# The first mixture's router stage in another order: expert loads and first splits earlier, token halves made there, slot weights summed between the gather's matmuls

## The chip, the cores and the metric

One core of a Trainium2 chip runs the whole program. The metric is the device time of one execution in microseconds (us). TensorE (PE) does matrix products, VectorE (DVE), ScalarE (ACT) and GpSimd (POOL) elementwise work, and SyncE (SP) issues the transfers.

## The reference

Two layers on 1024 tokens of 256 channels. The part around the change is the start of layer 0, cut here to what matters:

```
xn = layernorm(x)
s  = attention(xn, wq, wk, wv, wo)          # 16 heads of 128
# mixture of 32 experts, 4 per token, capacity C = 40 slots each
scores = sigmoid(xn @ router_w.T)
groups = top 3 of 8 groups by (scores + bias); idx = top 4 experts in them
w      = 2.5 * scores[idx] / sum(scores[idx])
Xp     = xn[slots_token]                    # (32 experts, 40 slots, 256)
Y      = (silu(Xp @ W_gate) * (Xp @ W_up)) @ W_down
out    = scatter_add(Y * slots_w) + (silu(xn @ shared_gate.T) * (xn @ shared_up.T)) @ shared_down.T
x      = x + s * silu(out)
```

## The kernel before

All operands stay in SBUF. Tokens lie on 128 partitions in 8 tiles (NT = 8). Products that need more than half precision are made of float16 halves: a value is split into a high half (a cast) and a low half (value minus high), and three products are summed.

The program is a row of blocks. In a block each engine has its own instruction stream, ordered by semaphores alone; at a block's end all five engines, SP too, meet at a barrier. Four blocks matter:

- **The first norm** (`layer_norm`, called from `route0` at L252): DVE normalizes, PE transposes `xn`, ACT copies the transposes to `xnT`. SP meanwhile issues five transfers (`load_first`, L247 to L251).
- **The router block** (L254 to L431). PE: `router_w` is turned, the logits follow (L273), the three shared weights are turned (L281), and four steps of the shared expert's gate and up products run (`shared_gate_up`, L292; a step is four float32 products, and the trace has two records for each). Two steps stand before the wait for `sel_ready`, then the counting products `pos` (L302, L303), then the other two steps. The gather (L316, L318) multiplies `xn` halves by the 0/1 matrix `member`, 12 products per token tile. The sums of slot weights `ws` (L325, L326, 160 small products) come last. DVE: one chain (`Chain`: each operation waits for the one before) computes the selection from `prob` (L389) to `sel16` (L407), then weights and places (L408 to L419), then the 8 tiles of `member` (L421), the low halves `xg_l` of the gathered tokens (L427) and the slot weights (L429, L431). ACT: sigmoid, copies of the turned weights, per shared step a Silu and a copy, and per expert of the first eight a high half and a scaled copy (`weights_high`, L343, L345). POOL: the halves of `xn` (L371, L373), per shared step a product `shared_hT` (L378), and per expert a low half (`weights_low`, L367). SP: 24 loads for experts 0 to 7 at the block's start, three for each of experts 8 to 15 once the buffer is free.
- **The expert block** (`experts0`): 32 experts; PE's products, ACT's `e_sg`, `e_hh`, and DVE's `e_hf`, `e_hl` follow each other per expert. POOL makes the halves of `xnT` for the attention that comes later (L559, L561); that is all it does there.
- **The combination** (`combine0`), and then the attention.

The order of work on each engine is written out by hand; nothing schedules it.

Of the kernel before, what the change touches and what calls it, by code (L numbers as in the profile page):

```python
# [7 lines left out]
ALU = mybir.AluOpType  # L8
ACT = mybir.ActivationFunctionType
# [4 lines left out]
NT = T // P  # L14
D = 256
DC = D // P
HALF = 512
# [12 lines left out]
ST = SLOTS // P  # L30
# [176 lines left out]
def route0(nc, env, router_w, e_bias):  # L207
# [6 lines left out]
    with ExitStack() as local:  # L214
# [20 lines left out]
        member_ready, gathered, xg_done, ws_ready, wm_done = (sem("r0_" + s) for s in ("me", "ga", "xg", "ws", "wm"))  # L235
        high_done, xn_split = (sem("r0_" + s) for s in ("hi", "xn"))
        wf, w_h, w_l, w_high, w_ready = (env[k] for k in ("wf", "w_h", "w_l", "w_high", "w_ready"))
# [9 lines left out]
        def load_first(sp):  # L247
            sp.dma_start(rw[:, :], router_w).then_inc(loaded[0], 16)
            sp.dma_start(bias[:, :], e_bias.partition_broadcast(P)).then_inc(loaded[1], 16)
            for i, src in enumerate(env["shared_weights"]):  # L250
                sp.dma_start(w3[i][:, :, :], src.rearrange("(a p) d -> p a d", p=P)).then_inc(w3_loaded[i], 16)  # L251
        layer_norm(nc, env, "ln0", env["x"], env["xn"], xnT, loads=load_first, side=env["fill_masks"])  # L252

        with nc.Block() as block:  # L254
            @block.sync
            def _(sp):

                for e in range(EB):
                    load_expert(sp, env, e, e)
                for b in range(EB):  # L260
                    sp.wait_ge(w_ready, b + 1)
                    load_expert(sp, env, EB + b, b)

            @block.tensor
            def _(pe):
# [29 lines left out]

                for step in range(2 * IC - 2):
                    shared_gate_up(step)
# [6 lines left out]
                last.then_inc(pos_ready, 1)  # L304
                for step in range(2 * IC - 2, 2 * IC):
                    shared_gate_up(step)

                pe.wait_ge(up_done, 2 * IC)
                pe.wait_ge(xn_split, 1)
                for n in range(NT):  # L310
                    pe.wait_ge(member_ready, n + 1)
                    for c in range(DC):
                        for k, (at, size) in enumerate(cuts):
# [6 lines left out]
                            if n == NT - 1:  # L320
                                last.then_inc(gathered, 1)
                for s in range(ST):
                    for n in range(NT):
                        slots = member[:, n, :, :].rearrange("p e c -> p (e c)")[:, s * P:(s + 1) * P]
                        pe.matmul(ws[:, s, :], slots, wk_h[:, n, :], start=(n == 0), stop=False)  # L325
                        last = pe.matmul(ws[:, s, :], slots, wk_l[:, n, :], start=False, stop=(n == NT - 1))  # L326
                last.then_inc(ws_ready, 1)

            @block.scalar
            def _(act):  # L330
                act.wait_ge(rwT_ready, 1)
                act.activation(rwT[:, :, :], turned, ACT.Copy).then_inc(rwT_done, 1)
                act.wait_ge(logits_ready, 1)
# [6 lines left out]
                def weights_high(e):  # L340

                    act.wait_ge(env["expert_loaded"][e], 48)
                    act.activation(w_h[e][:, :, :], wf[e][:, :, :], ACT.Copy, scale=WSCALE).then_inc(w_high, 1)  # L343
                    act.wait_ge(w_high, 2 * e + 1)
                    act.activation(wf[e][:, :, :], wf[e][:, :, :], ACT.Copy, scale=WSCALE).then_inc(w_high, 1)  # L345

                for step in range(2 * IC):
                    act.wait_ge(gu_ready, step + 1)
                    if step >= 2:
                        act.wait_ge(h_ready, step - 1)  # L350
                    bank = 2 * (step % 2)
                    act.activation(sg[:, step % 2, :], psum[:, bank, :], ACT.Silu).then_inc(silu_done, 1)
                    act.activation(up[:, step % 2, :], psum[:, bank + 1, :], ACT.Copy).then_inc(up_done, 1)
                    weights_high(step)
                for e in range(2 * IC, EB):
                    weights_high(e)
                for c in range(DC):
                    for k, (at, size) in enumerate(cuts):
                        bank = c * len(cuts) + k
                        act.wait_ge(gathered, bank + 1)  # L360
                        act.activation(xg_h[:, c, at:at + size], psum[:, bank, 0:size], ACT.Copy).then_inc(xg_done, 1)

            @block.gpsimd
            def _(pool):
                def weights_low(e):
                    pool.wait_ge(w_high, 2 * e + 2)
                    pool.tensor_tensor(w_l[e][:, :, :], wf[e][:, :, :], w_h[e][:, :, :], ALU.subtract).then_inc(w_ready, 1)  # L367
# [4 lines left out]
                pool.wait_ge(high_done, 1)  # L372
                pool.tensor_tensor(xn_l[:, :, :], xn[:, :, :], xn_h[:, :, :], ALU.subtract).then_inc(xn_split, 1)  # L373
                for step in range(2 * IC):
                    t, ic = step // IC, step % IC
                    pool.wait_ge(silu_done, step + 1)
                    pool.wait_ge(up_done, step + 1)
                    pool.tensor_tensor(hT[:, ic, t * HALF:(t + 1) * HALF], up[:, step % 2, :], sg[:, step % 2, :],  # L378
                                       ALU.mult).then_inc(h_ready, 1)
                    weights_low(step)  # L380
                for e in range(2 * IC, EB):
                    weights_low(e)

# [50 lines left out]
EB = 8  # L434
# [13 lines left out]
def experts0(nc, env):  # L448

    sem, psum, xg_h, xg_l, yT, wf, loaded = (env[k] for k in ("sem", "psum", "xg_h", "xg_l", "yT", "wf", "expert_loaded"))  # L450
    w_h, w_l, w_ready, xnT = (env[k] for k in ("w_h", "w_l", "w_ready", "xnT"))
    with ExitStack() as local:
        def tmp(name, shape, dt=F32):
# [3 lines left out]
        h_h, h_l = ([tmp(f"{n}{b}", [P, CAP], F16) for b in range(BANKS)] for n in ("hh", "hl"))  # L457
        wh_ready, gu_ready, silu_done, h_ready, hh_ready, hl_ready, y_ready, y_done, x_high = (
            sem("e0_" + s) for s in ("nwh", "gu", "si", "h", "hh", "hl", "y", "yd", "xh"))

# [13 lines left out]
        with nc.Block() as block:  # L474
# [57 lines left out]
            def _(dve):  # L532
# [20 lines left out]
                rounds(dve, (0, hidden, False), (3, next_low, True), (0, hidden_low, False), (3, outputs, False))  # L553

            @block.gpsimd
            def _(pool):

                high, low = env["xT_h"], env["xT_l"]
# [1654 lines left out]
```

## Time and profile before

| | |
|---|---|
| time, median of 3 runs | 1448.96 us (1448.11 to 1452.94) |
| span of the profiled execution, first to last instruction | 1450.3 us |
| router block, in that execution | about 15.1 to 73.2 us |
| expert block | from 73.5 us on |
| busy over the whole span | PE 87%, DVE 71%, ACT 50%, POOL 37% |

The profiled execution's own time is not listed apart from its span, which lies inside the range of the three runs and 1.3 us above their median. Times in the rows below count from the span's start.

### The profile page before, as it was taken

Reading aid. Unit: us, or ns where it says so; the run is one execution under the profiler, and the core shown is the slowest. Engines: PE = TensorE matmul, PEld = TensorE weight load, DVE = VectorE, ACT = ScalarE, POOL = GpSimd, SP = SyncE. Lnnn points to the kernel's source line nnn. Section 1 sums busy time; section 2 is a strip of 40 time slices with the busy share of each in tenths; the row PEclk is TensorE's granted clock in tenths of the full one; section 3 lists DMA queues with packets and bytes.
Section 4 is the critical chain, followed back from the end, with each engine's and each line's share of the span. In section 5 each row is a group of like instructions: output and inputs, shape, how many; then the busy total and the mean of one; then the engine's idle time right before and its main releaser. Section 6 shows DMA issues by size and latency. Waiting matters only on the chain. (4 is left out here: it accounts for less than half of the span.)

```text
span 1450.3 us, 25230 instructions
## 1 busy us (share of the span) xinstructions
PE 1258.0 (87%) x8970; PEld 764.3 (53%) x8970; DVE 1029.5 (71%) x1516; ACT 731.9 (50%) x1313; POOL 539.8 (37%) x333
## 2 busy tenths in 40 slices
PE   6857689988889988888998888796676999999997
PEld 4556556665665666565666547552233454444443
DVE  4785178998989998989998871459964425555554
ACT  3462376776676676676576641343035413434443
POOL 3612244546544545544454400034434003333332
PEclk9956899999999999999999999788888999999999
DMA  4351000000000000000000100103000024434441
GB/s 139 88 168 30 22 1 12 12 12 11 0 11 11 11 11 11 0 11 11 11 0 0 58 0 2 37 0 111 0 0 1 0 70 124 119 113 127 116 112 61
DMA packets 66543, 59.21 MB, mean 41 GB/s; under 512 B 7057, under 2 KB 61825, under 8 KB 66497
## 3 DMA queue, kind: packets, MB, share of 16 engines
q1 hardware_dynamic: 66496, 58.59, 14.1%
q8 instruction: 29, 0.48, 0.1%
q14 instruction: 18, 0.14, 0.0%
HBM read 57.26 MB, written 1.31 MB: 40 GB/s over the span
## 5 line engine op out<-in xcount | busy, mean ns | idle before, releaser
L1094 DVE SCALAR_TENSOR_TENSOR a_pr<-a_ex,a_rtot,a_pr 128x1024 f16<-128x1024 f32 x128 | 214.7, 1677 | 4.5
L1023 ACT COPY a_pT<-psum 128x1024 f32<-128x1024 f32 x128 | 130.6, 1020 | 93.6 <-PE psum L920 93.6
L1013 ACT ACTIVATE a_ex<-psum,a_nmax 128x1024 f32<-128x1024 f32 x128 | 144.9, 1132 | 65.2 <-DVE a_nmax L1079 65.2
L2074 POOL TENSOR_TENSOR e_sg<-e_sg,e_cb 128x512 f32<-128x512 f32 x64 | 82.0, 1282 | 242.2 <-ACT e_sg L2022 242.2
L1079 DVE TENSOR_REDUCE a_nmax<-psum 128x1 f32<-128x1024 f32 x128 | 155.4, 1214 | 19.6 <-PE psum L910 19.5
L1092 DVE TENSOR_SCALAR a_pr<-a_ex,a_rtot 128x1024 f16<-128x1024 f32 x128 | 161.8, 1264 | 5.1
L920 PE MATMUL psum<-ident,a_pr 128*128 128x128 f16 x2048 | 144.0, 227 | 24.2 <-DVE a_pr L1094 23.4
L920 PEld LDWEIGHTS psum<-ident,a_pr 128*128 128x128 f16 x2048 | 129.5, 102 | 42.0 <-DVE a_pr L1094 35.7
L851 POOL TENSOR_TENSOR a_qkTl<-a_qkTf,a_qkTh 128x512 f16<-128x512 f32 x64 | 93.1, 1473 | 100.6 <-ACT a_qkTf L997 100.6
L892 PE MATMUL psum<-a_wh,xT_h 128*128 128x128 f16 (+1 forms) x512 | 114.6, 247 | 3.0 <-PEq L578 1.2
L831 POOL TENSOR_TENSOR a_rnorm<-a_ss,a_power 128x16 f32<-128x16 f32 x16 | 46.4, 2903 | 188.8 <-DVE a_ss L1071 188.8
L893 PE MATMUL psum<-a_wl,xT_h 128*128 128x128 f16 (+1 forms) x512 | 114.5, 247 | 0.0
L894 PE MATMUL psum<-a_wh,xT_l 128*128 128x128 f16 (+1 forms) x512 | 114.5, 247 | 0.0
L2030 ACT ACTIVATE e_hh<-e_hf 128x512 f16<-128x512 f32 x64 | 40.3, 630 | 143.4 <-DVE e_hf L2099 143.4
L935 PE MATMUL psum<-a_pT,a_vh 128*128 128x512 f16 x256 | 97.0, 379 | 1.1 <-ACT a_pT L1023 1.1
L1945 PE MATMUL psum<-xT_h,e_guh 128*128 128x512 f16 x256 | 97.0, 379 | 0.4 <-DVE e_hf L2099 0.4
L936 PE MATMUL psum<-a_pT,a_vh 128*128 128x512 f16 x256 | 97.0, 379 | 0.0
L937 PE MATMUL psum<-a_pT,a_vl 128*128 128x512 f16 x256 | 97.0, 379 | 0.0
L1947 PE MATMUL psum<-xT_h,e_gul 128*128 128x512 f16 x256 | 97.0, 379 | 0.0
L1946 PE MATMUL psum<-xT_l,e_guh 128*128 128x512 f16 x256 | 97.0, 379 | 0.0
L880 PE MATMUL psum<-ident,qk 128*128 128x128 f32 x256 | 42.0, 302 | 50.0 <-ACT a_qkTf L997 19.4
L906 PE MATMUL psum<-a_qkTh 128*128 128x512 f16 x256 | 80.3, 397 | 0.0
(355 smaller groups left out, 2991.4 us busy)
## 6 DMA issues: line engine op xcount, KB each, us to landing
e_cb<-comb_by_expert SPq DMA_DIRECT2D x64, 256.0 KB, 3.7
wf<-in_L_ffn_W_gate SPq DMA_DIRECT2D x32, 128.0 KB, 2.3
wf<-in_L_ffn_W_up SPq DMA_DIRECT2D x32, 128.0 KB, 2.4
wf<-in_L_ffn_W_down SPq DMA_DIRECT2D x32, 128.0 KB, 2.9
e_guf<-in_L_ffn_wg SPq DMA_DIRECT2D x32, 128.0 KB, 2.2
e_guf<-in_L_ffn_wu SPq DMA_DIRECT2D x32, 128.0 KB, 2.2
e_dnf<-in_L_ffn_wd SPq DMA_DIRECT2D x32, 128.0 KB, 2.1
a_wf<-in_L_attn_wq SPq DMA_DIRECT2D x16, 128.0 KB, 2.2
```

Source lines behind the costliest of these rows:

```text
L892: pe.matmul(dst, xh, wh, start=(c == 0), stop=False)
L893: pe.matmul(dst, xh, wl, start=False, stop=False)
L894: last = pe.matmul(dst, xl, wh, start=False, stop=(c == DC - 1))
L920: last = pe.transpose(out, pr[m % 2][:, part, k * P:(k + 1) * P], ident16[:, :])
L935: pe.matmul(out, v_h[b][:, k, :], ph, start=(k == 0), stop=False)
L936: pe.matmul(out, v_h[b][:, k, :], pl, start=False, stop=False)
L937: last = pe.matmul(out, v_l[b][:, k, :], ph, start=False, stop=(k == KT - 1))
L1013: act.activation(ex[m % 2][:, :], psum[:, bank:bank + 2, :].rearrange("p a b -> p (a b)"), ACT.Exp, bias=nmax[:, m % 2:m % 2 + 1], accum_o ...
L1023: act.copy(dst, src).then_inc(pT_ready, 1)
L1079: dve.tensor_reduce(nmax[:, m % 2:m % 2 + 1], psum[:, bank:bank + 2, :].rearrange("p a b -> p (a b)"), AX.X, ALU.max, negate=True).then_in ...
L1092: dve.tensor_scalar(pr[k][:, 0, :], ex[k][:, :], rtot[:, k:k + 1], None, ALU.mult).then_inc(ph_ready, 1)
L1094: dve.scalar_tensor_tensor(pr[k][:, 1, :], ex[k][:, :], rtot[:, k:k + 1], pr[k][:, 0, :], ALU.mult, ALU.subtract).then_inc(p_ready, 1)
```

## The change

- The 24 loads of experts 0 to 7 are issued in the first norm's block, behind its five transfers.
- In the router block ACT splits expert 0 (high half) and makes `xT_h` before the sigmoid, and splits experts 1 and 2 before the first shared step; the other splits move up by three experts.
- POOL makes the low half of expert 0, then `xT_l` in four pieces of 512, then the low halves of experts 1 and 2, before the first shared product. The expert block loses both POOL operations.
- PE runs three shared steps before the counting products, and one after.
- The slot weight sums are made per token tile behind that tile's gather products.

```diff
 # route0, load_first (in the first norm's block)
                 sp.dma_start(w3[i][:, :, :], src.rearrange("(a p) d -> p a d", p=P)).then_inc(w3_loaded[i], 16)
+            for e in range(EB):
+                load_expert(sp, env, e, e)
 # router block, SP
-                for e in range(EB):
-                    load_expert(sp, env, e, e)
 # PE
-                for step in range(2 * IC - 2):
+                for step in range(2 * IC - 1):
                     shared_gate_up(step)
                 pe.wait_ge(sel_ready, 1)
...
-                for step in range(2 * IC - 2, 2 * IC):
-                    shared_gate_up(step)
+                shared_gate_up(2 * IC - 1)
...
-                for s in range(ST):
-                    for n in range(NT):
+                    for s in range(ST):
-                        pe.matmul(ws[:, s, :], slots, wk_h[:, n, :], start=(n == 0), stop=False)
+                        pe.matmul(ws[:, s, :], slots, wk_h[:, n, :], start=(n == 0 and s == 0), stop=False)
 # ACT
+                weights_high(0)
+                act.activation(env["xT_h"][:, :, :], xnT[:, :, :], ACT.Copy).then_inc(xT_high, 1)
                 act.wait_ge(logits_ready, 1)
...
+                weights_high(1)
+                weights_high(2)
                 for step in range(2 * IC):
...
-                    weights_high(step)
-                for e in range(2 * IC, EB):
-                    weights_high(e)
+                    weights_high(3 + step)
+                weights_high(EB - 1)
 # POOL
+                weights_low(0)
+                pool.wait_ge(xT_high, 1)
+                for c in range(DC):
+                    for half in range(2):
+                        at = (slice(None), c, slice(half * HALF, (half + 1) * HALF))
+                        pool.tensor_tensor(env["xT_l"][at], xnT[at], env["xT_h"][at], ALU.subtract)
+                weights_low(1)
+                weights_low(2)
                 for step in range(2 * IC):
...
-                    weights_low(step)
-                for e in range(2 * IC, EB):
-                    weights_low(e)
+                    weights_low(3 + step)
+                weights_low(EB - 1)
 # experts0, POOL
-                pool.tensor_copy(high[:, :, :], xnT[:, :, :]).then_inc(x_high, 1)
-                pool.wait_ge(x_high, 1)
-                pool.tensor_tensor(low[:, :, :], xnT[:, :, :], high[:, :, :], ALU.subtract)
```

SP's queue around the barrier between the norm's block and the router block, before (the branch that waits for the barrier opens the router block; `wf` are the experts' weights):

```order
L251 DMA r_w<-in_L_ffn_shared_down 128x2x256
L144 UNCONDITIONAL_BRANCH
L255 UNCONDITIONAL_BRANCH [waits barrier_Pool_Activation_PE_DVE_SP_release]
L442 DMA wf<-in_L_ffn_W_gate 128x256
L442 DMA wf<-in_L_ffn_W_up 128x256
```

The same place now, with the last six of the 24 expert loads ahead of the barrier:

```order
L449 DMA wf<-in_L_ffn_W_gate 128x256
L449 DMA wf<-in_L_ffn_W_up 128x256
L451 DMA wf<-in_L_ffn_W_down 128x256
L449 DMA wf<-in_L_ffn_W_gate 128x256
L449 DMA wf<-in_L_ffn_W_up 128x256
L451 DMA wf<-in_L_ffn_W_down 128x256
L144 UNCONDITIONAL_BRANCH
L257 UNCONDITIONAL_BRANCH [waits barrier_Pool_Activation_PE_DVE_SP_release]
```

So 24 transfers that were issued behind the barrier are issued ahead of it.

POOL's queue from the router block's start, before (`wl` are the experts' low halves; the expert block begins at L555):

```order
L371 CAST xn_h<-xn 128x2048
L373 TENSOR_TENSOR xn_l<-xn,xn_h 128x2048
L378 TENSOR_TENSOR shared_hT<-r_up,r_sg 128x512
L367 TENSOR_TENSOR wl<-wf,wh 128x768
L378 TENSOR_TENSOR shared_hT<-r_up,r_sg 128x512
L367 TENSOR_TENSOR wl<-wf,wh 128x768
L378 TENSOR_TENSOR shared_hT<-r_up,r_sg 128x512
L367 TENSOR_TENSOR wl<-wf,wh 128x768
L378 TENSOR_TENSOR shared_hT<-r_up,r_sg 128x512
L367 TENSOR_TENSOR wl<-wf,wh 128x768 x5
```

And now:

```order
L371 CAST xn_h<-xn 128x2048
L373 TENSOR_TENSOR xn_l<-xn,xn_h 128x2048
L367 TENSOR_TENSOR wl<-wf,wh 128x768
L379 TENSOR_TENSOR xT_l<-xnT,xT_h 128x512 x4
L367 TENSOR_TENSOR wl<-wf,wh 128x768 x2
L386 TENSOR_TENSOR shared_hT<-r_up,r_sg 128x512
L367 TENSOR_TENSOR wl<-wf,wh 128x768
L386 TENSOR_TENSOR shared_hT<-r_up,r_sg 128x512
L367 TENSOR_TENSOR wl<-wf,wh 128x768
```

Seven operations (three `wl`, four pieces of `xT_l`) now stand between `xn_l` and the first `shared_hT`, where nothing stood.

PE's queue around the counting products, as a difference:

```order
 L273 MATMUL psum<-r_rwT,xnT 128x32 x16
 L281 MATMUL psum<-ident,r_w 128x128 x12
-L292 MATMUL psum<-xnT,shared_wT 128x512 x8
+L292 MATMUL psum<-xnT,shared_wT 128x512 x12
 L303 MATMUL psum<-r_sel,upper 128x32
 L302 MATMUL psum<-r_sel,ones 128x32
```

Four products, one shared step, moved ahead of the counting products.

## Rows read from the trace of the kernel before

**Rows 1.** Busy time by stage: us, engine busy (instructions), granted clock, DMA share, GB/s.

```profile
50.60:68.00 17.40, 17.36 (x98) 9.46 (x99) 12.29 (x7) 9.44 (x14) 16.04 (x7) 1.00 0.39 115
...
80.00:120.00 40.00, 24.88 (x516) 21.65 (x514) 33.86 (x115) 27.12 (x82) 0.00 (x0) 0.50 0.53 159
```

**Rows 2.** Timeline, start of the router block: start, duration, engine, operation [idle before].

```profile
6.94 0.47 SPq L251 DMA_DIRECT2D r_w<-in_L_ffn_shared_down  x1
...
13.98 0.81 ACT L175 ACTIVATE xnT<-psum 128x256 f32<-128x256 f32 x2 [0.41 <-PE psum L190]
15.06 0.34 SPq L442 DMA_DIRECT2D wf<-in_L_ffn_W_gate  x1
...
17.05 4.06 POOL L373 TENSOR_TENSOR xn_l<-xn,xn_h 128x2048 f16<-128x2048 f32 x1
...
25.88 0.43 SPq L444 DMA_DIRECT2D wf<-in_L_ffn_W_down  x1
```

**Rows 3.** Timeline, ACT before the sigmoid.

```profile
22.88 0.39 ACT L334 ACTIVATE r_prob<-psum 128x256 f32<-128x256 f32 x1 [5.83 <-PE psum L273]
```

**Rows 4.** Timeline, DVE and POOL while the selection is computed.

```profile
33.63 1.27 POOL L378 TENSOR_TENSOR shared_hT<-r_up,r_sg 128x512 f32<-128x512 f32 x1 [12.52 <-ACT r_up L353]
...
34.25 0.69 DVE L201 COPY r_named<-r_best 128x32 f32<-128x32 f32 x1
...
37.34 1.13 DVE L204 TENSOR_SCALAR r_sel<-r_er 128x256 f32<-128x256 f32 x1
...
38.60 1.70 POOL L367 TENSOR_TENSOR wl<-wf,wh 128x768 f16<-128x768 f32 x1 [0.28 <-ACT wf L345]
38.72 1.87 DVE L408 TENSOR_TENSOR r_w<-r_prob,r_sel 128x256 f32<-128x256 f32 x1
```

**Rows 5.** One line's instructions, `member` and `wl`: shortest, median and longest in ns.

```profile
L421 DVE TENSOR_TENSOR member<-r_place,steps x8: 1481/2554/2932, 44.1 to 59.0; 128x1280 f16<-128x1280 f32 x8
...
L367 POOL TENSOR_TENSOR wl<-wf,wh x8: 1632/2296/2894, 35.2 to 65.0; 128x768 f16<-128x768 f32 x8
```

**Rows 6.** Timeline, three places of DVE's chain.

```profile
23.30 0.43 DVE L389 TENSOR_TENSOR r_sc<-r_prob,r_bias 128x256 f32<-128x256 f32 x1 [11.51 <-ACT r_prob L334]
...
24.99 0.23 DVE L396 TENSOR_TENSOR r_lo<-r_sums 128x64 f32<-128x64 f32 x1
...
44.14 17.80 DVE L421 TENSOR_TENSOR member<-r_place,steps 128x1280 f16<-128x1280 f32 x8
```

**Rows 7.** Timeline, PE: shared steps, counting products, gather and slot weight sums.

```profile
26.14 9.65 PE L292 MATMUL psum<-xnT,shared_wT 128*128 128x512 f32 x16 [0.69 <-ACT shared_wT L337]
...
38.86 0.21 PE L303 MATMUL psum<-r_sel,upper 128*128 128x32 f16 x1 [3.06 <-DVE r_sel L407]
...
39.84 9.62 PE L292 MATMUL psum<-xnT,shared_wT 128*128 128x512 f32 x16
...
50.64 0.39 PE L316 MATMUL psum<-member,xn_h 128*128 128x512 f16 x1 [1.18 <-ACT r_up L353]
...
67.96 0.18 PE L325 MATMUL psum<-wk_h,member 128*128 128x32 f16 x1
...
71.93 0.18 PE L326 MATMUL psum<-wk_l,member 128*128 128x32 f16 x1
```

**Rows 8.** Stretches around the counting products; columns as in group 1.

```profile
40.00:42.00 2.00, 2.00 (x4) 0.97 (x4) 1.83 (x6) 0.00 (x0) 0.30 (x1) 0.50 0.21 65
...
44.00:46.00 2.00, 2.00 (x5) 0.85 (x4) 1.97 (x3) 0.00 (x0) 0.00 (x0) 0.78 0.00 0
```

**Rows 9.** Timeline, DVE at the router block's end.

```profile
67.05 3.14 DVE L427 TENSOR_TENSOR xg_l<-psum,xg_h 128x512 f16<-128x512 f32 x6 [5.11 <-ACT xg_h L361]
...
72.67 0.49 DVE L431 TENSOR_REDUCE w_slot<-r_wmask 128x10 f32<-128x320 f32 x1
```

**Rows 10.** Timeline, POOL and DVE in the expert block.

```profile
75.43 4.06 POOL L561 TENSOR_TENSOR xT_l<-xnT,xT_h 128x2048 f16<-128x2048 f32 x1
...
75.94 3.60 DVE L540 TENSOR_TENSOR e_hl<-e_hf,e_hh 128x40 f16<-128x40 f32 x1 [0.30 <-ACT e_hh L522]
```

More of the change, by code:

```diff
@@ L235, in route0 @@
         member_ready, gathered, xg_done, ws_ready, wm_done = (sem("r0_" + s) for s in ("me", "ga", "xg", "ws", "wm"))
-        high_done, xn_split = (sem("r0_" + s) for s in ("hi", "xn"))
+        high_done, xn_split, xT_high = (sem("r0_" + s) for s in ("hi", "xn", "xh"))
         wf, w_h, w_l, w_high, w_ready = (env[k] for k in ("wf", "w_h", "w_l", "w_high", "w_ready"))
@@ L321, in _ @@
                                 last.then_inc(gathered, 1)
-                for s in range(ST):
-                    for n in range(NT):
+                    for s in range(ST):
                         slots = member[:, n, :, :].rearrange("p e c -> p (e c)")[:, s * P:(s + 1) * P]
-                        pe.matmul(ws[:, s, :], slots, wk_h[:, n, :], start=(n == 0), stop=False)
-                        last = pe.matmul(ws[:, s, :], slots, wk_l[:, n, :], start=False, stop=(n == NT - 1))
+                        pe.matmul(ws[:, s, :], slots, wk_h[:, n, :], start=(n == 0 and s == 0), stop=False)
+                        last = pe.matmul(ws[:, s, :], slots, wk_l[:, n, :], start=False, stop=(n == NT - 1 and s == ST - 1))
                 last.then_inc(ws_ready, 1)
@@ L332, in _, with weights_high @@
                 act.activation(rwT[:, :, :], turned, ACT.Copy).then_inc(rwT_done, 1)
+                def weights_high(e):
+                    act.wait_ge(env["expert_loaded"][e], 48)
+                    act.activation(w_h[e][:, :, :], wf[e][:, :, :], ACT.Copy, scale=WSCALE).then_inc(w_high, 1)
+                    act.wait_ge(w_high, 2 * e + 1)
+                    act.activation(wf[e][:, :, :], wf[e][:, :, :], ACT.Copy, scale=WSCALE).then_inc(w_high, 1)
+                weights_high(0)
+                act.activation(env["xT_h"][:, :, :], xnT[:, :, :], ACT.Copy).then_inc(xT_high, 1)
                 act.wait_ge(logits_ready, 1)
@@ L338, in _ @@
                                    ACT.Copy).then_inc(wT_done, 1)
[L340 to L345, printed above, removed]
+                weights_high(1)
+                weights_high(2)
                 for step in range(2 * IC):
@@ L450, in experts0 @@
     sem, psum, xg_h, xg_l, yT, wf, loaded = (env[k] for k in ("sem", "psum", "xg_h", "xg_l", "yT", "wf", "expert_loaded"))
-    w_h, w_l, w_ready, xnT = (env[k] for k in ("w_h", "w_l", "w_ready", "xnT"))
+    w_h, w_l, w_ready = (env[k] for k in ("w_h", "w_l", "w_ready"))
     with ExitStack() as local:
@@ L457, in experts0 @@
         h_h, h_l = ([tmp(f"{n}{b}", [P, CAP], F16) for b in range(BANKS)] for n in ("hh", "hl"))
-        wh_ready, gu_ready, silu_done, h_ready, hh_ready, hl_ready, y_ready, y_done, x_high = (
-            sem("e0_" + s) for s in ("nwh", "gu", "si", "h", "hh", "hl", "y", "yd", "xh"))
+        wh_ready, gu_ready, silu_done, h_ready, hh_ready, hl_ready, y_ready, y_done = (
+            sem("e0_" + s) for s in ("nwh", "gu", "si", "h", "hh", "hl", "y", "yd"))
         def rounds(engine, *jobs):
@@ L553, in _ @@
                 rounds(dve, (0, hidden, False), (3, next_low, True), (0, hidden_low, False), (3, outputs, False))
-            @block.gpsimd
-            def _(pool):
-                high, low = env["xT_h"], env["xT_l"]
-                pool.tensor_copy(high[:, :, :], xnT[:, :, :]).then_inc(x_high, 1)
-                pool.wait_ge(x_high, 1)
-                pool.tensor_tensor(low[:, :, :], xnT[:, :, :], high[:, :, :], ALU.subtract)
 def combine0(nc, env):
```

## The prediction, made before the changed kernel ran

> **What bounds the kernel now.** I read the busy time by stage first, then the timeline of each engine through the router block. The whole program is serial by blocks, so a microsecond in the router block or in the expert block is one of the total. In the router block the bound changes hands. First PE: from the barrier to the sigmoid's inputs, for which ACT sat idle 5.83 us [rows 3]. Then DVE's selection chain, from 23.3 to 38.8 [rows 4, 6]: PE stood idle 3.06 us before the counting products because `sel16` wasn't there [rows 7]. Then PE again: two shared steps of 9.62 us in all, at first at the lower clock, a wait of 1.18 us for ACT, then the gather from 50.64 to 67.96 and the slot weights to 71.96 [rows 7]; the stage row shows PE busy 17.36 of 17.40 us and DVE with room [rows 1]. A short DVE tail ends the block at 73.16 [rows 9]. In the expert block one DVE operation of 40 columns took 3.60 us [rows 10].
>
> **Term 1, the barrier: +3.9.** SP meets the barrier too. Its last transfer of the norm's block was issued by 7.41, and the barrier fell when ACT was through at 14.79; the next block began at 15.06, 0.27 later [rows 2]. The 24 loads took from 15.06 to 26.31, 0.469 us each [rows 2]. Behind 7.41 they end at 7.41 + 24 x 0.469 = 18.7, so the router block begins at about 19.0 and not at 15.06: +3.9 us. Nothing of it comes back by itself: no engine in the router block waited for an expert load before (the waits there are for PE and for DVE [rows 3, 7]). If SP issued faster ahead of a barrier, the least is 0; the most is the row's value.
>
> **Term 2, work put ahead of the sigmoid on ACT: 0.** The split of expert 0 and `xT_h` lie in ACT's idle 5.83 us before the sigmoid [rows 3], with the table load: I estimate some 1.7 + 2.0 us. Experts 1 and 2 are split while PE does shared step 0. Without that cover the first would cost 3.7 us.
>
> **Term 3, POOL against DVE: +10.5.** This is the large one. The timeline of both engines [rows 4] shows that certain DVE operations do not run beside a POOL operation: the copy of 32 columns begun at 34.25 took 0.69 us and ended with POOL's product (34.90); `r_sel` took 1.13 us; the product begun at 38.72 took 1.87 us and ended just after POOL's `wl` (40.30). The subtraction of 40 columns in the expert block lasted until POOL's 4.06 us operation was over [rows 10]. When both queues are full they take turns: the longest `member` is 2.93 against 1.48 us for the shortest, so one `wl` of 1.63 us costs DVE 1.45 [rows 5], 0.89 of its length.
>
> Now POOL had nothing between 21.11 and 33.63 [rows 2, 4], just where DVE's chain begins. After the change, with everything 3.9 later, `xn_l` ends at 25.0, `wl` of expert 0 at 26.7, and then four pieces of `xT_l` follow (about 1.15 us each, between a quarter of the 4.06 and the 1.27 of another operation on 512 columns [rows 10, 4]), then two `wl`. DVE's chain begins at 27.2, and its first six operations, 23.30 to 25.22 before [rows 6], each have two inputs in SBUF. Each waits for one POOL operation and lets the next one in when it ends: 0.6 us of the first piece, 3 x 1.0 for the others, 2 x 1.45 for the `wl` of experts 1 and 2 (ready at about 31.7 and 33.4, POOL comes to them at 32.0 and 33.7): 6.5 us.
>
> The rest of the chain is now later against the shared steps. PE's steps 0, 1 and 2 end at 36.2, 39.7 and 43.1 ([rows 7], 3.9 later, the third step at the faster half's pace of about 3.4 us), so POOL has `shared_hT` and `wl` three times between 37.6 and 47.6. DVE's maxima and match operations run through; stepping through the others I find five waits: 1.0, 1.05, 1.2, 0.9 and 1.3 us, together 5.4. All six POOL operations by 0.89 of their lengths would be 7.7, none 0. Taken away are the old waits of this kind before `sel16`: 0.5 and 0.85 us [rows 4]. So `sel16` is ready at 38.8 + 3.9 + 6.5 + 5.4 - 1.35 = 53.2. The bounds of this term: -1.35, if nothing contends any more, and +12.9.
>
> The Trainium skill bears on this, in "SBUF — State Buffer", section "Who interferes with whom": a VectorE instruction with two SBUF inputs and a GpSimd instruction that reads SBUF exclude each other for the whole instruction. The rows agree that they exclude each other; with the whole length in place of 0.89 of it, the sum would be 1.3 us higher.
>
> **Term 4, the shared step moved: -3.4.** Step 2 fills PE until 43.1, then PE is idle ten microseconds. The counting products take 1.0 us as before (38.86 to 39.84 [rows 7]), to 54.2. Before, after 3.06 us of idling, the granted clock was 0.50, 1.2 GHz, and 0.78 as a mean at 44 to 46 [rows 8], and two steps took 9.62 us, where at 2.4 GHz they would be twice 3.4. After a longer idle time I expect the same start: one step of 6.2 us, 3.4 less than the two (about 6.4 of its 8 records at the slow pace of 0.86 us). It ends at 60.4. The wait for ACT stays 1.2: the gather begins at 61.6 instead of 50.64. `member` doesn't hold it: the chain from 38.72 to 44.14 [rows 4, 6] is 1.45 us shorter without the old wait, so the tiles start at 57.2 and the third is ready by 61.5.
>
> **Term 5, slot weights beside the gather: +1.5.** PE had to do 17.3 us of gather and 4.0 of slot weights [rows 7]; interleaved it does the same 21.3, since `member`'s tiles come faster than the 2.66 us it then needs for one. Gather and sums end at 82.9. What changes is the tail. Before, DVE's `xg_l`, 3.14 us long and ended at 70.19, lay beside the slot weight sums, which ended at 71.96, and the block ended 1.2 later at 73.16 [rows 7, 9]. `xg_l` ended 4.4 us after the last tile's gather began (a tile is 17.3 / 8 = 2.17 us, so that was at 65.8). Now that tile begins 2.67 before PE's end, so `xg_l` ends 1.7 after it, and the two slot weight operations of 0.49 us each follow: 2.75. The block ends at 85.7 against 73.16: +12.5. Were PE waiting for `member`, the sums would be free and this term would be a gain of up to 2.5.
>
> **Term 6, the expert block: -3.4.** Without POOL's subtraction the 3.60 us operation takes 0.2, as its like do [rows 10]. DVE is the busiest engine there, 33.86 of 40 us [rows 1], and the whole pipeline starts by that much earlier. Least 0, most 4.1.
>
> **Sum.** 3.9 + (6.5 + 5.4 - 1.35) gives `sel16` 14.4 later; PE gets back 3.4 (one step less behind it), gathers 11.0 later, ends 1.5 later in the tail (12.5), and gains 3.4: +9.1 us. The span of the profiled execution, 1450.3, would be 1459.4; the three runs have a median 1.3 lower, so I predict 1449.0 + 9.1 = 1458.1, and 0.6% slower.
>
> **Rivals.**
> *The contention is small (chance 0.13; on the other side).* If DVE's short operations pass between POOL's, `sel16` comes at 38.8 + 3.9 - 1.35 = 41.4, before PE is through with step 2 at 43.1. Then PE never idles: counting to 43.8, step 3 to 47.2, gather from 48.4 to 69.7, end at 72.4. With the expert block that is -0.8 - 3.4 = -4.2: 1444.8. For it: the maxima and match operations don't wait. Against it: every overlap of the two engines that I looked at [rows 4, 5, 10]. It decides from the point where all waits together stay under about 2 us: `sel16` by 43.4 gives a gather at 51.8 even with a slow step 3, and at most no loss.
> *Half of it (0.16).* POOL's operations fall beside maxima and match operations more than I stepped: waits of 6 us. `sel16` at 47.3, PE cold, gather from 55.7, the end at 79.8: +6.6 - 3.4 = +3.2: 1452.2, with a spread of 1450.5 to 1455.
> *The clock in the expert block (0.06).* It is 0.50 from 80 to 120 [rows 1] and fell beside the stall that goes. Should it stay at 2.4 GHz, the block can shrink until DVE is full, by at most 40.0 - 33.9 = 6.1: 1452.0. Against it: PE is not the bound there, and its idle time before that block grows from 1.9 to over 3 us. With little contention as well it would be 1439; I count half of the 0.06 for each.
>
> **How the numbers follow.** The main case has 0.65 and its own range is 1455 to 1462 (terms 3 and 4 each off by 2 to 3). From 1450 to 1462 I take in the half case and most of the clock case, and leave out the rival on the other side: 0.8 in all. What a measurement can tell from no change is about 0.3%, 4.3 us, so from 1444.6 to 1453.3. Slower: the main case and half of the half case, 0.65 + 0.08 = 0.73. Faster: 0.08 of the small contention, which lies at the very bound, and 0.03 of the clock case, 0.11. Within: the rest, 0.16.
>
> **What would show it.** The router block's first operation at 19.0 and not 15.1. `r_sc`, `r_hi`, `r_lo` and their kind each at 1.0 to 1.8 us instead of 0.3, with POOL's `xT_l` ending where they end. The counting products near 54, after a PE idle time of some ten microseconds, and slow records in step 3. The gather from about 61.6 and 21.3 us long, `xg_l` behind PE's end. The `e_hl` group without its 3.60. The prediction is wrong if DVE's first six operations keep their 0.3 us, if SP's issues are not waited for, or if PE waits for `member` tile by tile.

## The result, and the profile after

| | before | changed |
|---|---|---|
| median (range) of 15 runs each | 1448.56 us (1445.40 to 1453.73) | 1455.13 us (1453.35 to 1456.37) |
| span of the profiled execution | 1450.3 | 1452.6 |

The ratio is 1.0037, 95% interval 1.0026 to 1.0047: the changed kernel is slower by 5.4 us (3.8 to 6.8). The medians lie 6.6 us apart; the means of the same runs, 1449.49 and 1454.93 us, 5.4. Predicted were 9.1 us and a time of 1458.1, with a range of 1450 to 1462.

The two spans differ by 2.3 us only. One line's instructions in the attention show where the two executions part. These are ACT's copies `sq`, in the kernel before:

```profile
L985 ACT ACTIVATE sq<-psum x64: 597/597/605, 164.3 to 798.7; 128x512 f32<-128x512 f32 x64
```

and in the changed one:

```profile
L984 ACT ACTIVATE sq<-psum x64: 597/597/604, 170.0 to 801.9; 128x512 f32<-128x512 f32 x64
```

The attention starts 5.7 us later and ends 3.2 later, with the same code. Over all thirteen traces of this study the same distance runs from 631.9 us (the changed kernel has this) to 634.8; before has 634.4. So an execution can lose or gain up to 2.9 us there for no cause in the kernel. I compare the stages ahead of the attention in the traces, and the totals by the ratio.

Start of the router block after the change, timeline of SP, POOL and ACT:

```profile
18.41 0.43 SPq L451 DMA_DIRECT2D wf<-in_L_ffn_W_down  x1
19.25 1.89 POOL L371 CAST xn_h<-xn 128x2048 f16<-128x2048 f32 x1 [11.74 <-POOLq L144]
21.23 4.07 POOL L373 TENSOR_TENSOR xn_l<-xn,xn_h 128x2048 f16<-128x2048 f32 x1
25.25 1.64 POOL L367 TENSOR_TENSOR wl<-wf,wh 128x768 f16<-128x768 f32 x1
...
26.85 4.78 POOL L379 TENSOR_TENSOR xT_l<-xnT,xT_h 128x512 f16<-128x512 f32 x4
...
27.06 0.39 ACT L341 ACTIVATE r_prob<-psum 128x256 f32<-128x256 f32 x1 [2.42 <-PE psum L273]
...
31.96 3.25 POOL L367 TENSOR_TENSOR wl<-wf,wh 128x768 f16<-128x768 f32 x2 [0.33 <-ACT wf L336]
```

Against [rows 2] the barrier falls 4.2 us later, behind SP's last issue; POOL's 7.55 us of idle time in the norm's block became 11.74. ACT still idles 2.42 us for PE before the sigmoid [rows 3]: what was put there is hidden.

DVE's chain in the same timeline:

```profile
27.48 0.81 DVE L396 TENSOR_TENSOR r_sc<-r_prob,r_bias 128x256 f32<-128x256 f32 x1 [15.70 <-ACT r_prob L341]
28.32 1.13 DVE L399 TENSOR_TENSOR r_hi<-r_sc 128x128 f32<-128x128 f32 x1
29.49 1.12 DVE L400 TENSOR_TENSOR r_lo<-r_sc 128x128 f32<-128x128 f32 x1
30.65 1.13 DVE L401 TENSOR_TENSOR r_sums<-r_hi,r_lo 128x128 f32<-128x128 f32 x1
31.81 0.23 DVE L402 TENSOR_TENSOR r_lo<-r_hi 128x64 f32<-128x64 f32 x1
32.07 1.61 DVE L403 TENSOR_TENSOR r_lo<-r_sums 128x64 f32<-128x64 f32 x1
...
33.98 1.30 DVE L405 TENSOR_TENSOR r_gs<-r_lo 128x64 f32<-128x64 f32 x1
...
40.99 4.47 DVE L411 TENSOR_TENSOR r_es<-r_sc,r_gm 128x64 f32<-128x64 f32 x4
...
50.76 0.29 DVE L414 CAST r_sel<-r_sel 128x256 f16<-128x256 f32 x1
...
54.94 15.29 DVE L428 TENSOR_TENSOR member<-r_place,steps 128x1280 f16<-128x1280 f32 x8
```

`r_hi`, `r_lo` and `r_sums` took 0.29 us each before and take 1.13 now, nearly as long as one piece of `xT_l` (4.78 us for four). The one operation of the six that kept its 0.23 is the one that came while POOL idled 0.33 us for ACT. `sel16` is ready at 51.05, 12.25 us later than before [rows 4].

PE's timeline, against [rows 7]:

```profile
30.32 10.57 PE L292 MATMUL psum<-xnT,shared_wT 128*128 128x512 f32 x24 [0.69 <-ACT shared_wT L344]
51.11 0.21 PE L303 MATMUL psum<-r_sel,upper 128*128 128x32 f16 x1 [10.22 <-DVE r_sel L414]
...
52.10 4.59 PE L292 MATMUL psum<-xnT,shared_wT 128*128 128x512 f32 x8
...
57.87 0.39 PE L315 MATMUL psum<-member,xn_h 128*128 128x512 f16 x1 [1.18 <-DVE member L428]
...
79.17 0.18 PE L324 MATMUL psum<-wk_l,member 128*128 128x32 f16 x1
```

PE idles 10.22 us for `sel16` and gathers 7.2 us later than before. Gather and sums take 21.5 us together, as before. Busy time and granted clock of the changed kernel in three stretches around the last step, and at the end one in the expert block (columns as in [rows 1]; the clock column, the third from the end, is 0.50 at 1.2 GHz and 1.00 at 2.4 GHz):

```profile
50.00:52.00 2.00, 0.89 (x33) 0.89 (x34) 1.83 (x8) 0.00 (x0) 0.00 (x0) 0.50 0.00 0
52.00:54.00 2.00, 2.00 (x13) 0.97 (x10) 1.83 (x6) 0.00 (x0) 0.00 (x0) 0.51 0.00 0
54.00:56.00 2.00, 2.00 (x6) 0.91 (x5) 1.90 (x4) 0.00 (x0) 0.00 (x0) 1.00 0.00 0
...
88.00:128.00 40.00, 25.20 (x493) 21.79 (x491) 32.45 (x110) 25.91 (x78) 0.13 (x2) 0.50 0.55 165
```

DVE's tail and the expert block, against [rows 9, 10]:

```profile
77.79 3.15 DVE L434 TENSOR_TENSOR xg_l<-psum,xg_h 128x512 f16<-128x512 f32 x6 [7.55 <-ACT xg_h L361]
...
81.36 0.49 DVE L438 TENSOR_REDUCE w_slot<-r_wmask 128x10 f32<-128x320 f32 x1
...
84.73 0.20 DVE L547 TENSOR_TENSOR e_hl<-e_hf,e_hh 128x40 f16<-128x40 f32 x1 [0.30 <-ACT e_hh L529]
...
127.54 0.48 DVE L635 TENSOR_SCALAR c_yw_h<-psum,w_slot 128x256 f16<-128x256 f32 x1 [2.01 <-PE psum L599]
```

The block ends at 81.85 instead of 73.16; the 3.60 us operation is 0.20. The last row is the combination's first DVE operation. It began at 121.94 before. So up to there the change costs 5.6 us in these two executions, which is the size of the measured difference.

### The profile page after: what moved, and what is told of

Its sections match the earlier page's. It is cut to its first block and busy times, and to the rows that moved or that the text cites. A ratio compares the mean times of both kernels' runs of the same rounds, so it can differ in the third digit from the quotient of the medians.

```text
span 1452.6 us, 25233 instructions
## 1 busy us (share of the span) xinstructions
PE 1249.9 (86%) x8970; PEld 761.9 (52%) x8970; DVE 1034.3 (71%) x1516; ACT 733.8 (51%) x1314; POOL 531.8 (37%) x335
## 5 line engine op out<-in xcount | busy, mean ns | idle before, releaser
L1091 DVE TENSOR_SCALAR a_pr<-a_ex,a_rtot 128x1024 f16<-128x1024 f32 x128 | 165.9, 1296 | 5.1
L919 PE MATMUL psum<-ident,a_pr 128*128 128x128 f16 x2048 | 143.2, 226 | 24.1 <-DVE a_pr L1093 23.4
L830 POOL TENSOR_TENSOR a_rnorm<-a_ss,a_power 128x16 f32<-128x16 f32 x16 | 46.4, 2902 | 190.4 <-DVE a_ss L1070 190.4
L879 PE MATMUL psum<-ident,qk 128*128 128x128 f32 x256 | 42.4, 304 | 49.9 <-ACT a_qkTf L996 19.4
L2098 DVE SCALAR_TENSOR_TENSOR e_hf<-psum,e_sg 128x512 f32<-128x512 f32 x64 | 43.8, 684 | 50.3 <-POOL e_sg L2073 50.3
```

The source lines that it names most:

```text
L919: last = pe.transpose(out, pr[m % 2][:, part, k * P:(k + 1) * P], ident16[:, :])
L1091: dve.tensor_scalar(pr[k][:, 0, :], ex[k][:, :], rtot[:, k:k + 1], None, ALU.mult).then_inc(ph_ready, 1)
```

## The experiments

The places that tell the runs apart, in us from each span's start. "Combination" is the first `c_yw_h`; the ratio is to runs of the kernel before on the same chip, with its 95% interval. Ten or more runs stand behind each ratio, but only five behind the last one. The places are of one execution each.

| kernel | chain starts | sel16 | member starts | block ends | combination | ratio |
|---|---|---|---|---|---|---|
| before | 23.3 | 38.8 | 44.1 | 73.2 | 121.9 | 1 |
| changed | 27.5 | 51.05 | 54.9 | 81.9 | 127.5 | 1.0037 (1.0026, 1.0047) |
| before + loads early | 27.5 | 42.8 | 48.1 | 77.1 | 125.8 | 1.0027 (1.0010, 1.0043) |
| changed, loads back | 23.4 | 47.3 | 51.2 | 79.0 | 124.05 | 1.0007 (0.9996, 1.0019) |
| changed, xT_l out | 27.5 | 46.4 | 50.3 | 77.5 | 123.2 | 1.0002 (0.9987, 1.0017) |
| changed, splits back | 27.5 | 46.0 | 51.3 | 77.6 | 123.2 | 1.0003 (0.9990, 1.0016) |
| changed, loads back, xT_l out | 23.7 | 44.2 | 48.1 | 76.2 | 121.1 | 0.9984 (0.9975, 0.9993) |
| before + sums beside | 23.3 | 38.1 | 43.4 | 73.0 | 121.8 | 0.9998 (0.9985, 1.0011) |
| before + step moved | 23.3 | 38.7 | 48.3 | 75.8 | 124.6 | 0.9992 (0.9979, 1.0005) |
| before + xT out | 23.3 | 39.05 | 44.4 | 71.8 | 116.75 | 0.9971 (0.9952, 0.9991) |
| the same, again | 23.3 | 40.7 | 44.6 | 74.5 | 120.2 | 0.9984 (0.9972, 0.9996) |
| mix | 23.3 | 41.6 | 45.5 | 73.1 | 118.2 | 0.9980 (0.9965, 0.9995) |
| mix, low halves late | 23.3 | 39.7 | 43.6 | 70.5 | 116.2 | 0.9955 (0.9942, 0.9969) |

The theory after the result: the barrier costs 4.2 us, POOL's operations ahead of and among DVE's chain cost more than that, and a gain in PE's steps and in the expert block gives a part back. The rival: the loads or the clock made the chain or PE late, and POOL is a bystander.

**The loads alone (kernel before).**

```diff
 # load_first
                 sp.dma_start(w3[i][:, :, :], src.rearrange("(a p) d -> p a d", p=P)).then_inc(w3_loaded[i], 16)
+            for e in range(EB):
+                load_expert(sp, env, e, e)
 # router block, SP
-                for e in range(EB):
-                    load_expert(sp, env, e, e)
```

> The kernel before with one edit: the 24 expert loads are issued in the first norm's block. If SP's issues hold the barrier, the router block's first POOL operation starts at 19.3 us instead of 15.07 and everything behind it keeps its distances: the combination's first DVE operation comes at 126.1 instead of 121.9, the time is 4.2 us longer. The rival, that earlier loads give something back (a split, or the loads of experts 8 to 15, that came late before), expects under 2 us.

The router block began at 19.25, and every later place lies 3.9 to 4.2 us behind that of before, to the combination. The ratio's middle is 3.9 us (1.4 to 6.2). Nothing came back in the trace: the barrier theory holds there, and the rival's bound of 2 us does not. The ratio alone would not exclude it.

**The changed kernel with the loads back.** The same edit in reverse.

> The changed kernel with the 24 loads back behind the barrier. By the barrier theory 4.2 us less than the changed kernel: the router block starts at 15.1, the combination's first DVE operation at about 123.4 instead of 127.5, and what is left of the loss against before is 1.4 us. ACT's first split must now wait for expert 0 to land (about 18.5), which its idle time before the sigmoid holds. The rival, that the early loads carry the early splits, expects no gain.

The block began at 15.08 and the combination at 124.05, 3.5 us earlier than in the changed kernel, where 4.2 were expected. The three shared steps ahead of the counting products took 13.20 us here and 10.57 there, the last one 5.47 and 4.59. In the last step here the granted clock was still 0.51 at 50 to 52, up to 3.7 us behind its start. In the first three the profile shows 1.00 all along in both runs, yet from 28 to 30 this run has four records in 2 us, where six are the full pace: what slowed them, the clock column doesn't show. The early split used up its cover: ACT waited 2.39 us for expert 0's last load, from 15.75 to 18.14, and with `xT_h` and the table load behind it the sigmoid came 0.1 us late (0.4 in the run with both edits, below). So of the rival's idea, that the early loads carry the early splits, 0.1 to 0.4 us are real. The ratios, 1.0007 against 1.0037 with intervals that don't overlap, agree that the early loads were a loss.

**The changed kernel with `xT_l` in the combination.**

```diff
 # router block, POOL
-                pool.wait_ge(xT_high, 1)
-                for c in range(DC):
-                    for half in range(2):
...
-                        pool.tensor_tensor(env["xT_l"][at], xnT[at], env["xT_h"][at], ALU.subtract)
 # combine0
-            block.gpsimd(env["head_weights"].split_first)
+            @block.gpsimd
+            def _(pool):
+                env["head_weights"].split_first(pool)
+                pool.tensor_tensor(env["xT_l"][:, :, :], env["xnT"][:, :, :], env["xT_h"][:, :, :], ALU.subtract)
```

> The changed kernel with POOL's four pieces of xT_l taken out of the router block and done as one operation in the combination, behind the head weights' split (ACT still makes xT_h in the router block). If POOL's operations make DVE's chain wait turn by turn, DVE's first six operations fall to 0.3 us each, the match operations run until about 34, and only the later expert halves still meet the chain: sel16 at about 46.5 instead of 51.05, the gather 4 us earlier, the combination at 123 to 124. The rival, that the chain is late for another cause than POOL, leaves sel16 near 51.

DVE's timeline in this run:

```profile
27.93 0.29 DVE L394 TENSOR_TENSOR r_hi<-r_sc 128x128 f32<-128x128 f32 x1
28.25 0.29 DVE L395 TENSOR_TENSOR r_lo<-r_sc 128x128 f32<-128x128 f32 x1
...
34.15 1.06 DVE L204 TENSOR_SCALAR r_gm<-r_gr 128x64 f32<-128x64 f32 x1
...
35.70 3.60 DVE L406 TENSOR_TENSOR r_es<-r_sc,r_gm 128x64 f32<-128x64 f32 x4
...
46.14 0.29 DVE L409 CAST r_sel<-r_sel 128x256 f16<-128x256 f32 x1
```

The first operations are back at 0.29 us, `sel16` is ready at 46.4 and the combination begins 4.35 us earlier. POOL is the cause, not a bystander; what is left of the waits (1.06, 3.60) are the expert halves and shared products. The ratio, 1.0002, has an interval that lies wholly below the changed kernel's.

**The changed kernel with the splits in their old places.**

```diff
 # ACT
-                weights_high(0)
...
-                weights_high(1)
-                weights_high(2)
...
-                    weights_high(3 + step)
+                    weights_high(step)
 # POOL likewise with weights_low
```

> The changed kernel with the expert splits on ACT and POOL in their old places, while the loads, the four pieces of xT_l and the rest stay changed. POOL's pieces then follow xn_l from 25.3 to 30.1 and meet DVE's chain from 27.5: two or three waits, about 2.3 us, and behind them the waits of before. sel16 at 45.5 to 47 instead of 51.05, the combination at 123 to 124 instead of 127.5. If only xT_l mattered in the changed kernel, sel16 would stay near 50.

`sel16` at 46.0, the combination at 123.2: as expected. DVE's first two operations met two pieces of `xT_l` and took 1.44 and 1.13 us; the rest of the six ran at 0.23 to 0.29. So the two parts of POOL's new work are about equal: taking either away gives 4.6 to 5.1 us back at `sel16` and 4.3 at the combination. With the 3.5 us of the loads either would make up for more than the whole loss of 5.6; the next run tests that.

**The changed kernel without early loads and without `xT_l` in the router block.** The two edits together.

> The changed kernel without its two large costs: loads behind the barrier (4.2 us) and xT_l in the combination (4.3). If the two add up, the combination starts at about 119.2 instead of 127.5, and the time is 2 to 3 us less than before. If one hid a part of the other, as the shared steps' clock suggests, it starts at 120 to 121.

The combination begins at 121.1, not 119.2: 6.5 us less than the changed kernel, where the two edits alone gave 3.5 and 4.35, together 7.85. The 1.4 us are missing before the counting products: `sel16` came 6.8 us earlier, where the two alone gave 3.75 and 4.6. PE's last step is not the reason. It took 1.2 us more than in the changed kernel (5.78 against 4.59), but in the two runs alone it took 0.9 and 0.3 more, which is as much. DVE's chain tells where POOL's operations fell this time:

```profile
28.00 1.45 DVE L201 COPY r_named<-r_best 128x24 f32<-128x24 f32 x1
...
32.35 4.04 DVE L406 TENSOR_TENSOR r_es<-r_sc,r_gm 128x64 f32<-128x64 f32 x4
```

With `xT_l` out alone the first of these took 0.18 us and the second 3.60; the operation behind `r_es` took 1.58 here and 1.22 there, the copy behind that 1.12 and 0.80, and only `r_gm` gained (0.20 for 1.06). That is 1.5 us more of waits. So how much a POOL operation costs depends on which DVE operation it meets, and the prices of single edits don't add up. The ratio (0.9984, up to 0.9993) is on the gaining side.

**The slot weight sums alone (kernel before).**

```diff
-                for s in range(ST):
-                    for n in range(NT):
+                    for s in range(ST):
...
```

> The kernel before with one edit: the slot weight sums are made per token tile behind that tile's gather. If PE is the bound of the gather and the sums only laid a cover over DVE's tail, gather and sums still take 21.3 us, and from PE's last sum to the router block's last DVE operation it is 2.7 us instead of 1.2: 1.5 us longer in the block. The rival, that PE waits for member between tiles, expects the sums to be free: the block up to 2.5 us shorter.

The gather begins at 49.02 and the block ends at 72.99, 23.97 us later; before it was 73.16 - 50.64 = 22.52. So the same work takes 1.45 us more, as the tail theory says, and the rival (sums for free) is out for this order of steps. The ratio shows nothing (its interval is -2.2 to +1.6 us), and the combination is where it was, because in this execution the four shared steps happened to take 1.56 us less (8.90 and 8.81 us for two each, against 9.65 and 9.62).

**The shared step alone (kernel before).**

```diff
-                for step in range(2 * IC - 2):
+                for step in range(2 * IC - 1):
                     shared_gate_up(step)
...
-                for step in range(2 * IC - 2, 2 * IC):
-                    shared_gate_up(step)
+                shared_gate_up(2 * IC - 1)
```

> The kernel before with one edit: three shared steps before the counting products and one behind. PE fills its 3.06 us of idle time, the counting products start at 39.3 to 39.6 instead of 38.86, the last step runs at 2.4 GHz in 3.4 us and ends near 43.8 instead of 49.46. But POOL's third shared product and expert half now come at 40.4 to 43.4, where DVE's chain computes the places: member starts 1 to 2 us later, and PE then waits for member's tiles at 1.4 us each and 2.85 beside POOL. I expect the gather to begin at 47 and the block to end 0.5 to 1.5 us earlier. The rival, that PE alone sets the gather's start, expects 4 to 5 us.

A miss: the block was expected 0.5 to 1.5 us shorter. PE did what was expected: the last step ran at full speed, 3.68 us, and ended at 43.57. But DVE and POOL in this run:

```profile
41.99 1.88 DVE L411 SCALAR_TENSOR_TENSOR r_w<-r_w,r_winv 128x256 f32<-128x256 f32 x1
44.82 0.42 DVE L416 TENSOR_TENSOR r_w<-r_w,r_keep 128x256 f32<-128x256 f32 x1
...
48.34 16.96 DVE L420 TENSOR_TENSOR member<-r_place,steps 128x1280 f16<-128x1280 f32 x8
```

```profile
40.42 1.27 POOL L377 TENSOR_TENSOR shared_hT<-r_up,r_sg 128x512 f32<-128x512 f32 x1 [0.17 <-ACT r_up L352]
41.95 1.64 POOL L366 TENSOR_TENSOR wl<-wf,wh 128x768 f16<-128x768 f32 x1 [0.27 <-ACT wf L344]
...
44.84 1.54 POOL L377 TENSOR_TENSOR shared_hT<-r_up,r_sg 128x512 f32<-128x512 f32 x1 [1.24 <-ACT r_up L352]
46.38 11.97 POOL L366 TENSOR_TENSOR wl<-wf,wh 128x768 f16<-128x768 f32 x5
```

POOL's later products all came earlier and met the end of the chain: `member` started 4.2 us later than before, the gather at 51.30, 0.7 later, and the block ended 2.6 later. The other 2.0 us are PE's own, in the gather and the sums:

```profile
51.30 0.59 PE L315 MATMUL psum<-member,xn_h 128*128 128x512 f16 x1 [7.73 <-DVE member L420]
```

```profile
50.00:52.00 2.00, 0.70 (x2) 0.29 (x3) 2.00 (x2) 1.94 (x4) 2.00 (x1) 0.50 0.81 226
52.00:54.00 2.00, 2.00 (x7) 0.91 (x6) 2.00 (x2) 0.73 (x1) 2.00 (x2) 0.50 0.30 80
```

PE had idled 7.73 us for the first tile. The granted clock, 1.00 at 46 to 48, fell to a mean of 0.54 at 48 to 50 meanwhile, and the gather began at 1.2 GHz. Its first ten products took 3.7 us, where they took 1.95 before at a granted clock of 1.00; that is 1.8 us of it. So an earlier PE step made POOL collide with DVE, and the wait for DVE cost PE its clock. This is one execution: the ratio over ten, 0.9992 (0.9979 to 1.0005), shows no loss in the whole. Where `sel16` is very late, as in the changed kernel, POOL's work of the first three steps is done before the chain's end, and the moved step shortens the way from `sel16` to the gather.

**`xT` alone in the combination (kernel before), twice.**

```diff
 # experts0
-            @block.gpsimd
-            def _(pool):
...
-                pool.tensor_copy(high[:, :, :], xnT[:, :, :]).then_inc(x_high, 1)
-                pool.wait_ge(x_high, 1)
-                pool.tensor_tensor(low[:, :, :], xnT[:, :, :], high[:, :, :], ALU.subtract)
 # combine0, behind split_first
+                pool.tensor_copy(high[:, :, :], xnT[:, :, :]).then_inc(x_high, 1)
+                pool.wait_ge(x_high, 1)
+                pool.tensor_tensor(low[:, :, :], xnT[:, :, :], high[:, :, :], ALU.subtract)
```

> The kernel before with both POOL operations on xnT (xT_h, xT_l) moved from the expert block to the combination, behind the head weights' split, and nothing else. The 3.60 us operation e_hl becomes 0.2 and the expert block 3.3 us shorter: the combination at 118.6 instead of 121.9, the time 1445.3. The rival, that the expert loads or the clock set that block's length, expects under 1 us of gain; a rival for the combination, that POOL there holds up DVE or the end of the block (barrier near 164), expects the gain to be lost there.

> The kernel before with xT alone in the combination, again and on the same chip as the version above: 3.3 us less than before by the expert block, ratio 0.997 to 0.998.

No `e_hl` above 0.20 us. From the expert block's first `e_hl` to the combination it took 42.7 and 43.4 us, against 121.94 - 75.32 = 46.6 before: the stall was worth 3.2 us or a little more. The rest of the difference between the two executions of one and the same kernel (116.75 and 120.2) is in the router block: its shared steps took 9.89 and 8.05 us in the one, 7.13 and 9.05 in the other, and in the second the early steps put POOL's products onto DVE's `r_es`, so `sel16` came at 40.7. Both ratios are under 1. The rival, that the gain is lost in the combination, is out: from its first DVE operation to the attention's first `sq` it is 41.9 and 42.0 us, against 42.4 before.

**The mix: before, with `xT` out, the moved step and the sums beside the gather.**

> The kernel before with xT_h and xT_l in the combination, three shared steps before the counting products, and the slot weight sums beside the gather; loads and expert splits as before. Where PE waits for member, the sums beside the gather cost nothing: 3.3 us from the expert block and 2 to 3 from the router block, combination at 116 to 117 against 121.9 of before. The rival, that the sums only move the tail, expects no more than the version with xT alone gave.

The combination at 118.2 instead of 116 to 117. `sel16` was late (41.6), once more by POOL's products and low halves: `r_es` took 2.16 us and not 1.20, the operation behind it 1.57 and not 0.29. As in the second execution above, the first steps had the full pace from their start, so that POOL's first product came at 31.11 and not at 33.63. Not better than `xT` alone.

**The mix with the experts' low halves behind the shared products.**

```diff
 # ACT: expert 0 before the sigmoid, the others one step earlier
+                weights_high(0)
                 act.wait_ge(logits_ready, 1)
...
-                    weights_high(step)
+                    weights_high(1 + step)
 # POOL
                 pool.tensor_tensor(xn_l[:, :, :], xn[:, :, :], xn_h[:, :, :], ALU.subtract).then_inc(xn_split, 1)
+                weights_low(0)
...
-                    weights_low(step)
-                for e in range(2 * IC, EB):
+                for e in range(1, EB):
                     weights_low(e)
```

> The mix of the version before (xT in the combination, three shared steps ahead of the counting products, sums beside the gather, loads behind the barrier), and now POOL splits expert 0 before DVE's chain begins, makes the four shared products alone, and the low halves of experts 1 to 7 behind them, where DVE builds member. If the waits of DVE's chain are POOL's expert halves, sel16 is ready before 39.5, member starts near 44 instead of 45.5 in the mix and 48.3 with the steps alone, the gather near 45.5, the router block ends near 70.6 against 73.16 of before, and the combination starts near 116. Together with the expert block that is 5 to 6 us less than before. If the waits only move to member and PE waits there, no better than xT alone, 3 to 4 us less than before.

POOL's queue in this run:

```profile
37.97 1.26 POOL L378 TENSOR_TENSOR shared_hT<-r_up,r_sg 128x512 f32<-128x512 f32 x1 [2.16 <-ACT r_up L352]
46.63 2.40 POOL L378 TENSOR_TENSOR shared_hT<-r_up,r_sg 128x512 f32<-128x512 f32 x1 [7.40 <-ACT r_up L352]
48.98 17.50 POOL L366 TENSOR_TENSOR wl<-wf,wh 128x768 f16<-128x768 f32 x7
```

`member` starts at 43.60, the gather at 46.54, the block ends at 70.53, the combination starts at 116.2, all close to what was expected. The median is 1443.02 us against 1448.14 for before on that chip, the ratio 0.9955 (0.9942 to 0.9969): 6.5 us less than before (4.5 to 8.4). It is the lowest ratio of the study, but over five runs, and its interval overlaps those of the mix and of the first run with `xT` alone. Against the mix the pair is a clean one up to `sel16`: in both the first three steps took 10.57 us and POOL's first product came at 31.11. `sel16` is 1.9 us earlier, because the operation behind `r_es` took 0.29 us and not 1.57, and the copy behind that 0.62 and not 1.25. Another 0.7 us of the gather's 2.6 are the last step, 4.62 us for 5.30. The expert halves are as many as ever; they now wait against `member`, of which PE has enough in store.

## Why the prediction was right, and where its sizes were off

The direction, the mechanisms and the range were right. The size was 9.1 us for 5.4 (5.6 in the trace up to the combination), and the median of 1455.13 lies at the very edge of the main case's own range of 1455 to 1462.

- **Term 1, the barrier, 3.9.** Right: 4.2 in the trace, 3.9 by the loads alone in the combination's start.
- **Term 2, ACT's work, 0.** Right: ACT idled 2.42 us where it had 5.83, at no cost.
- **Term 3, POOL against DVE, 10.5.** Mis-sized: 12.25 - 4.2 = 8.05. In the first stretch I let each of six operations wait (6.5). It was 4.3: the three whole waits for pieces of `xT_l` cost 0.84 us each and not 1.0, and the fifth operation slipped through while POOL waited 0.33 us for ACT. The second `wl` then met `r_gs` for 1.07, which makes 5.3 for the stretch. For the shared products and the expert halves behind them I had 5.4; it was 4.0 (0.76 at `r_gm`, 3.27 at `r_es`). Less the 1.35 of before, the waits make 8.0. PE's first three steps ended at 40.9 and not at 43.1, because they had the full pace from their start, and POOL was through at 45.3, before the copy and `r_sel`, which met nothing. How much of the 1.4 us this made is open; the run with the loads back had slow first records and a chain only 0.3 us longer. That POOL causes it is shown by the two runs that take away either part of its work. The Trainium skill's rule ("SBUF — State Buffer", section "Who interferes with whom"), exclusion for the whole instruction, agrees with these rows in kind; priced by POOL's whole length per wait the sum would have erred further. The waits are not confined to operations with two inputs: `r_gm`, which reads one tensor, took 0.95 us instead of 0.19.
- **Term 4, the moved step, -3.4.** Mis-sized, -5.0: the gather came 7.2 us later where `sel16` came 12.25 later. The last step took 4.59 us and not 6.2; the granted clock was 1.00 from 54 on, two microseconds after the step's start, where before it was 0.78 as a mean at 44 to 46, four to six microseconds after. A part of this is luck: in the six runs where the last step began at 0.50 it took 4.59 (here), 4.62, 4.88, 5.30, 5.47 and 5.78 us. In two others PE was at 1.00 when it began, and it took 3.68. No run puts the step back in the changed kernel, so the -5.0 is read from the two traces alone; in the run with the step alone the gather began no earlier but 0.7 us later.
- **Term 5, the sums beside the gather, +1.5.** Right: 1.45 in the run with the sums alone, 8.69 - 7.23 = 1.46 in the changed kernel.
- **Term 6, the expert block, -3.4.** Nearly: 3.1, from the block's end (8.7 later) to the combination (5.6 later), and 3.2 or a little more with that edit alone.

The measured terms are 4.2 + 8.05 - 5.0 + 1.45 - 3.1 = 5.6, most of them read from the same two executions. Of the 3.5 us too many, 2.5 are term 3 and 1.6 term 4, less 0.6 by which terms 1 and 6 were too kind. Of the rivals, small contention is refuted by DVE's rows, and the clock did not stay up in the expert block (0.50 from 88 to 128). The rival "half of it" is not far off either: the waits were 9.4 us, between its 6 and my 11.9, but the loss of 5.4 us lies nearer to its 3.2 than to my 9.1, because terms 3 and 4 erred the same way. What is not settled is what sets the moment at which PE takes up its full pace in the shared steps (in the last ones the granted clock shows it, in the first ones it reads 1.00 at either pace). Two executions of one kernel, which differ in it, have their combinations 3.4 us apart, and no run here controlled it.

## What to carry to other kernels

A queue that only issues transfers also meets the block's barrier: work put ahead of a barrier must fit in the slack of that queue (SP had 7.4 us here and got 11.3 us of issues). Idle time of one engine is no free room if its operations exclude another engine's: POOL was idle from 21 to 34 us, but that was exactly where DVE's chain ran undisturbed. Put such work where the other engine has a store of finished results (`member`) or waits for PE and works from PSUM (in the combination, with `xT` there, the copy of `gate` at 133.53 took 0.42 us beside `xT_l`, as its like do without POOL), not where it runs a chain.

## What the runs showed that I had not expected

- Two engines that take turns make small operations as slow as the large ones beside them: 0.29 us became 1.13, three times in a row, and four operations on 64 columns took 4.47 us instead of 1.20.
- An earlier PE step made the block 2.6 us longer in one execution: POOL got its inputs earlier and met DVE, and PE, idle for 7.73 us, began the gather at 1.2 GHz. 1.8 us of the loss are the clock.
- The prices of two edits, 3.5 and 4.35 us alone, made 6.5 together, because POOL's operations met other operations of DVE's chain.
- The same two shared steps at the same place took 7.13, 8.90, 9.47, 9.65 and 9.89 us in different executions. The trace of one execution can be off by 1 to 3 us at a place behind them, and the ratios over ten runs tell the total to 1.3 to 2.8 us.
